# Experts of a mixture: GpSimd's scatter chooses its rows by slot 64 in place of slot 128

## The reference, cut to what matters

```python
scores = jax.nn.softmax(logits, axis=-1)
_, topk_idx = jax.lax.top_k(scores + bias[None, :], K)         # K = 8 of 64
w = w / (w.sum(-1, keepdims=True) + EPS) * SCALE
routed = topk_idx < E                                          # E = 32
...
gu = jnp.einsum('ech,ehf->ecf', buf, w_gate_up)                # up to CAP = 256 tokens of each expert
g, u = jnp.split(gu, 2, axis=-1)
act = jax.nn.silu(g) * u
y = jnp.einsum('eci,eih->ech', act, w_down)
...
routed_out = jnp.einsum('tk,tkh->th', w_r, y_exp)
out = routed_out * (1.0 + w_z.sum(-1, keepdims=True))
```

## Time and profile before

| | us |
|---|---|
| median of three runs | 997.62 (997.1 to 997.64) |
| time of the profiled execution | 999.98 |
| its span, first to last instruction | 998.2 |
| TensorE busy | 909.7 |
| VectorE busy | 771.1 |
| ScalarE busy | 503.7 |
| GpSimd busy | 487.7 |
| GpSimd's scatters, 38 of them | 71.4 |

### The profile page before, as it was taken

One profiled execution on the slowest core, in us unless ns is written; L12 is line 12 of the kernel. 1 busy time (PEld: TensorE's weight loads), 2 busy tenths in 40 slices (PEclk: granted clock), 3 DMA queues, 4 the chain that ended last, 5 costly groups with the idle time before them and its releaser, 6 DMA issues. The chain is left out here.

```text
span 998.2 us, 14510 instructions
## 1 busy us (share of the span) xinstructions
PE 909.7 (91%) x4362; PEld 734.8 (74%) x4362; DVE 771.1 (77%) x1837; ACT 503.7 (50%) x867; POOL 487.7 (49%) x394
## 2 busy tenths in 40 slices
PE   5789999999999999999979999999978999797980
PEld 3577888888888888888758888888756767575860
DVE  6978888888988888888877777777685887586740
ACT  5454655555555465554562332332235887576740
POOL 1456766666766666676610000000025665676652
PEclk9989999999999999999999999999989999898995
DMA  8011111111111111111844664432185999899753
GB/s 302 6 33 48 50 47 48 59 43 48 59 38 58 49 44 58 48 42 39 295 162 149 226 249 182 132 136 97 55 268 143 311 334 286 250 281 289 182 66 42
DMA packets 68824, 131.03 MB, mean 131 GB/s; under 512 B 11836, under 2 KB 14268, under 8 KB 66688
## 3 DMA queue, kind: packets, MB, share of 16 engines
q1 hardware_dynamic: 58144, 114.67, 32.9%
q0 software_dynamic: 10592, 15.29, 8.7%
HBM read 106.53 MB, written 35.91 MB: 143 GB/s over the span
## 5 line engine op out<-in xcount | busy, mean ns | idle before, releaser
L595 POOL TENSOR_TENSOR a_t<-a_t 128x512 f32<-128x512 f32 x80 | 105.0, 1313 | 101.9 <-DVE a_t L358 101.9
L604 POOL TENSOR_TENSOR a_fQ<-a_fQ,a_den 128x512 f32<-128x512 f32 x64 | 87.9, 1374 | 71.9 <-DVE a_den L396 71.9
L213 PE MATMUL a_PQ<-w_h,a_xT_h 128*128 128x512 f32 x384 | 107.9, 403 | 10.0 <-DVE w_l L345 9.3
L782 PE MATMUL r_PY<-w_h,r_o_h 128*128 128x512 f32 x256 | 106.3, 415 | 3.4 <-DVE r_o_l L884 3.4
L1222 POOL DMA_INDIRECT out<-m_y,si x38 | 71.4, 1879 | 77.4 <-DMA out<-m_y,si 65.0
L1072 POOL TENSOR_SCALAR r_vr<-r_mv 128x1 f32<-128x1 f32 x16 | 8.4, 524 | 199.0 <-DVE r_mv L895 199.0
L213 PE MATMUL a_PQ<-w_l,a_xT_h 128*128 128x512 f32 x384 | 104.3, 394 | 0.0
L213 PE MATMUL a_PQ<-w_h,a_xT_l 128*128 128x512 f32 x384 | 103.5, 392 | 0.0
L782 PE MATMUL r_PY<-w_l,r_o_h 128*128 128x512 f32 x256 | 101.8, 398 | 0.0
L782 PE MATMUL r_PY<-w_h,r_o_l 128*128 128x512 f32 x256 | 101.8, 398 | 0.0
L392 DVE CUSTOM_DVE_ANT_0 a_m<-a_fQ,a_z 128x128 f32<-128x128 f32 x256 | 100.4, 444 | 0.0
(11 more groups left out here) (183 smaller groups left out, 2258.2 us busy)
## 6 DMA issues: line engine op xcount, KB each, us to landing
oT<-a_o SPq DMA_DIRECT2D x64, 256.0 KB, 2.4
v_l<-in_wgu SPq DMA_DIRECT2D x32, 512.0 KB
raw<-in_wgu SPq DMA_DIRECT2D x24, 512.0 KB
v_l<-oT SPq DMA_DIRECT2D x11, 1024.0 KB, 6.8
v_l<-in_wd SPq DMA_DIRECT2D x16, 512.0 KB
raw<-in_wd SPq DMA_DIRECT2D x12, 512.0 KB
v_h<-oT SPq DMA_DIRECT2D x5, 1024.0 KB, 6.6
out<-r_x SPq DMA_DIRECT2D x18, 256.0 KB, 2.0
```

Source lines behind the costliest of these rows:

```text
L213: last = eng.matmul(bank[:, :], a[:, k, :], w[:, 4 * i + k, :], start=s == 0 and k == 0, stop=s == 2 and k == 3)
L595: eng.tensor_tensor(t1[:, r % 2, :], t1[:, r % 2, :], t2[:, r % 2, :], ALU.add).then_inc(sm["xr"], 1)
L604: eng.tensor_tensor(q, q, den[:, n % 2, :].unsqueeze(2).broadcast_to([P, 4, P]), ALU.mult).then_inc(sm["fs"], 1)
L782: last = eng.matmul(PY[c % 2][:, :], a[:, c % 2, h * P:(h + 1) * P], b[:, h, :], start=h == 0 and s == 0, stop=h == NH - 1 and s == 2)
```

## The change

GpSimd no longer branches on slot 128 but on slot 64. An expert whose slot 64 is empty, one with up to 64 tokens, scatters 64 rows of its first tile and counts `m_s` up by 32; every other expert scatters both tiles with 128 rows each. An expert with 65 to 128 tokens therefore scatters its second tile too, whose slots are all dump rows. Slot 64 lies in partition 64 of `si`; GpSimd loads its flag from a small tile `full` in partition 0, into which VectorE copies that row of `si` behind its six memsets, and waits once for `m_full`. The other engines branch as before.

```diff
@@ experts
+        full = sb("full", [1, 64], U32)
...
+        def load_full(eng, regs, e):
+            eng.reg_load(regs[e % 7], full[0:1, 2 * e:2 * e + 1])
...
@@ GpSimd
-                def scatter(e, t, done):
+                def scatter(e, t, rows, done):
...
                     eng.indirect_dma_start(
-                        out[:, :], bass.IndirectOffsetOnAxis(ap=si[:, i:i + 1], axis=0),
-                        y[:, e % 4, t, :], None, compute_op=ALU.add).then_inc(sm["m_s"], done)
+                        out[:, :], bass.IndirectOffsetOnAxis(ap=si[0:rows, i:i + 1], axis=0),
+                        y[0:rows, e % 4, t, :], None, compute_op=ALU.add).then_inc(sm["m_s"], done)
...
-                    load_flag(eng, regs, e)
+                    if e == 0:
+                        eng.wait_ge(sm["m_full"], 1)
+                    load_full(eng, regs, e)
                     with eng.If_lt(regs[e % 7], T):
-                        scatter(e, 0, 16)
-                        scatter(e, 1, 16)
+                        scatter(e, 0, P, 16)
+                        scatter(e, 1, P, 16)
                     with eng.Else():
-                        scatter(e, 0, 32)
+                        scatter(e, 0, 64, 32)
@@ VectorE
                 for i in range(6):
                     clear(i)
+                eng.tensor_copy(full[:, :], si[64:65, :]).then_inc(sm["m_full"], 1)
                 w_low(1, (0, 1))
```

## The result

| | median us | ratio to before | 95% interval |
|---|---|---|---|
| before | 997.63 | | |
| changed | 981.35 | 0.9832 | 0.9815 to 0.985 |

The change takes 16.3 us off. The forecast was 968 with a range from 959 to 985, so the sign was right and the time lies in the range, but it lies outside the narrower 964 to 978, which had a chance of 0.61, and only a little over half of the 29.5 us gain arrived. In two later comparisons the same kernel came to 0.9834 (0.9799 to 0.9868) and 0.9822 (0.9784 to 0.9861).

What follows compares the result with a forecast made beforehand. One chain bounds the experts' stage: scatter issued, landed, next scatter issued. 12.5 + 4.0 + 18.1 - 2.6 - 2.5 = 29.5 us off the 998.2 span gives 968.7, less 0.6 is 968; range 959 to 985.

Steps and rivals of the forecast that it cites:

- loaded landing: Experts' stage under weight loads: shorter landings in 20 rounds, up to 1.2 us each where GpSimd waits, 18.1 us together.
- the rival of a fixed landing: Rival: 64-row scatters land no faster, only GpSimd's issue shrinks; 988 us, or 981 to 986 with slightly shorter landings; chance 0.17.
- The issue term: GpSimd's issue of 25 scatters, 64 rows fewer each: 0.5 us saved per scatter, 12.5 us, all on the chain.
- The quiet landing: Landings in five quiet rounds (experts 26, 28, 29, 30 and the end behind 31): 0.8 us less each, 4.0 us.
- The 2.5 us: Given back in six late rounds between the doubles of experts 18 and 25, as loads come closer together; bounds 0 to 7.2.
- Expert 15's pair: Expert 15 scatters twice instead of once in the experts' stage: 2.6 us added on the chain.
- Copy and flag at nothing: VectorE's 1 x 64 copy and GpSimd's wait and flag load: hidden by the first scatter's wait for y, no cost.
- The floor: Rival: the chain falls to 955 to 960 and TensorE, ending at 953.6, sets the end; time 959 to 964; chance 0.18.

Runs made afterwards that it cites:

- the pair alone: The changed kernel with its Else branch scattering 128 rows again, leaving the copy, the slot 64 flag and expert 15's second scatter: 1001.36 us, ratio 1.0024.
- the second branch: The changed kernel with a branch on slot 128 inside the first, so expert 15 scatters one 128-row tile: 980.22, 981.24 and 982.36 us.
- the three branches: The changed kernel with branches at slots 32, 64 and 128, nothing left out: 974.55 us (0.975) and 972.68 us (0.9755).
- the small gathers: The changed kernel with gathers of 16 indices, not 128, for the empty second tiles of 22 experts from 6 on: 982.59 us, 0.9861.

## Why half of the predicted gain came

**The mechanism held, and the range held by luck.** The chain of issue, landing and next scatter bounds the stage: with 64, 32 and 16 rows the time went 981, 975 and 972 us, and only rows of scatters were changed. But the terms of issue, loaded landing and pair were mis-sized, and the 981.35 lies outside the 964 to 978 of the forecast proper. It lies in 959 to 985 because that range took in the rival of a fixed landing (981 to 986), whose mechanism is refuted below.

**The issue term failed.** It was 25 x 0.5 = 12.5 us, reasoned from the 0.55 us between a gather and a scatter of equally many rows, which "can hardly be fixed". Nearly all of the issue is fixed. An undisturbed issue of 64 rows is 1.43 us, so the term should have been 25 x 0.12 = 3.0 us. The trace has 5.5 us less in the 25 issues together, since some issues take 2 to 2.7 us whatever their rows, and their number differs from one profile to the next. 7.0 us of the missing gain are here. The lower bound of that term, 0, was much nearer than the value taken. Of the 5.5 us some 2.5 are not the rows': with the pair alone, where all scatters have 128 rows again, the same 25 issues took 46.0 us against 48.3 before. The two other profiles of the changed kernel have 44.5 and 43.1 where this one has 42.8.

**The quiet landing held.** 4.0 us were said for five rounds. The four rounds and the end are 5.2 us shorter, 0.6 of it issue, so 4.6 us of landing, and 4.4 and 4.9 by the two other profiles of the changed kernel.

**The loaded landing was too large.** 18.1 - 2.5 = 15.6 us were said; the 20 rounds are 15.7 us shorter, but that has 4.9 us of issue in it, so the landing gave 10.8. The 2.5 us were charged for the six rounds between the pairs of experts 18 and 25, and there nothing was given back: their landings were to give 4.0 us before the charge and gave 4.1 (5.6 and 3.8 by the two other profiles). The gain is missing in the fourteen rounds before, of experts 2 to 17, where the transfers are densest (258 to 334 GB/s in the 20 us windows from 780 to 900, against 224 and 168 in the two behind): 14.1 us were said and 6.7 came (4.8 and 7.5 by the others), half a microsecond a round in place of one. Several of these rounds keep 7 us or more, which the prediction's last sentence names as a sign of being wrong: 7.95 us for expert 6's with a wait of 2.83 and 7.63 for expert 13's, while experts 4 and 3 went from 8.02 and 8.92 to 5.79 and 5.24. What holds the long ones was not tested. Of the thirteen waits that were credited with 1.2 us each, one (2.64 us, ahead of expert 6's scatter) is put down by the trace of before to VectorE and not to a landing.

**Expert 15's pair was too small in its round, and not in the time.** 2.6 us were taken from quiet pairs; under the loads its round became 5.4 us longer (4.8 and 4.4 by the two other profiles). Timed alone it costs 2.4 us (0.2 to 4.5), and leaving it out gained nothing clear in three comparisons. So the 5.4 us explain this trace and not surely the median.

**The sum by the trace.** -5.5 -4.6 -10.8 +5.4 -0.2 for the pairs makes, but for rounding, -15.6 us behind the first scatter, and -2.1 are ahead of it. The missing 13.9 us of 29.5 are, but for rounding, 7.0 of issue, 4.8 of loaded landing and 2.8 of the pair, less 0.6 in the quiet landing and 0.2 in the pairs. This is the account of one trace of each kernel; the two other profiles of the changed kernel differ from it by up to 3 us in a line of the table.

**Copy and flag at nothing:** nothing in the trace speaks against it. The first scatter still idles 6.8 us for y, and starts no later than before.

**The rivals.** A fixed landing is refuted by the quiet rounds, which lost 0.6 to 1.0 us beside their issue, and by data moving for 1.4 us in place of 2.2. That the measured time is nevertheless the one of this rival (981 to 986) came about by the other term, a nearly fixed issue. Here the rule of the Trainium skill (DMA: Bandwidth & Descriptors, section Anatomy of one DMA) doesn't agree with the trace: by bytes at 436 GB/s the 64 rows would be worth 0.3 us of landing, and the quiet round less its issue lost 0.6 to 1.0. The floor was not reached, but TensorE's end in it was right: 953.6 said, and with 32 rows the last matmuls start at 953.98 and end at 954.6. The time that goes with it is an estimate of 965 rather than 962, since the end behind the last scatter took 10 us in those runs.

**What the profile was to show:** 39 scatters (they are there); 1.05 us for a short one (wrong, 1.43); quiet rounds near 3.6 (3.82 to 4.18); waits for landings near 40 us (55.5); ScalarE's waits nearly gone (5.8 of 15.2, and 13.8 in another profile); TensorE's nearly gone (wrong, 10.6 of 14.0), and its low clock with them. That came only with 32 rows and fewer (0.9 to 1.2 us). In the changed kernel the clock still falls:

```profile
880.00:900.00 20.00, 15.33 (x63) 11.27 (x62) 14.00 (x17) 12.31 (x19) 11.15 (x9) 0.89 0.95 294
900.00:920.00 20.00, 15.19 (x59) 11.91 (x58) 11.23 (x14) 10.98 (x17) 13.93 (x10) 0.77 0.84 224
```

Four waits of TensorE for gathers, of 1.9 to 2.5 us, stand in these two windows. Two of them are followed by four transposes of 1.1 us together where 0.63 is usual.

## What to carry to other kernels

Before a smaller list is credited with a shorter issue, ask whether the issue goes by the list at all. Two operations of one size that differ in time show how the kinds differ, not how the size counts. Where only one size stands in the trace, the end of the range that says "fixed" deserves as much weight as the other. And a chain of small dependent transfers is worth shortening by rows as long as one engine has several of them: here down to 32 rows, which is 2 for each engine if they spread as the 64 did.

## What was not expected of the hardware

- The undisturbed issue of an indirect scatter that adds is 1.29 us for 16 rows and 1.55 for 128, that of a gather 0.90 for 16 indices and 1.00 for 128, also where all of them are empty slots.
- Of scatters alike in form some take 1.9 to 2.7 us to issue and not 1.4 to 1.6, with 16 rows (up to 2.40) as with 128. The traces show what they coincide with: VectorE splitting weights (L1122). Before and with the pair alone all 22 such issues overlap splits by about half a microsecond or more, and none of the 31 issues without overlap takes more than 1.83; in the three profiles of the changed kernel 30 of 35 long ones overlap. But 7 to 11 scatters in each profile overlap as much and stay short, and no run moved the splits, so it is not shown that they are the cause.
- SyncE's wait at the end of the program was 4.2 to 4.3 us before, in the changed kernel three times and with the pair alone, 6.1 to 6.4 with the second branch, 6.8 with the three branches, 6.4 with the small gathers, and 6.9 and 7.0 with 32 and 16 rows, although the last two have the changed kernel's instructions one by one. It eats 2 to 2.7 us of what these kernels gain. The row puts it down to TensorE's sequencer, but TensorE's last instruction had ended 14 us or more before the end. What ends last in all thirteen profiles, ahead of the closing semaphore events, is a DRAIN of GpSimd, 0.24 us before the end. Where the wait is short the end comes 4.5 us behind the last landing, where it is long 8.7 us behind the end of the last scatter's issue, whatever its rows. What decides between the two stays open.
